# A graph network on one core: inverse counts in the near rows, folds in place of a reduce, and three and two near tiles by turns

## What is computed

```python
x_j = node_features[col]                                   # 100000 x 16
m = silu(einsum('ei,ej,ijh->eh', x_j, edge_attr_8, W_msg_tp) / sqrt(16 * 8))
agg = segment_sum(m @ W_msg_lin / sqrt(16), row, n_nodes)
```

```python
cnt = zeros((num_nodes, 8)).at[dst, edge_type].add(1.0)
norm = 1.0 / maximum(cnt[dst, edge_type], 1.0)             # one number for each edge
agg = segment_sum(msg * norm[:, None], dst, num_nodes)
```

## Time and profile before

| | |
|---|---|
| median of three runs | 4680.27 us |
| the profiled execution, whole | 4656.31 us |
| its span | 4654.4 us |
| TensorE busy, matmuls | 4430.5 us (95%) |
| VectorE busy | 4185.4 us (90%) |
| ScalarE busy | 3232.3 us (69%) |
| GpSimd busy | 3395.2 us (73%) |
| mean granted clock of TensorE | 0.981 of full |

### The profile page before, as it was taken

How to read it: one execution, slowest core, us unless ns; L and a number is a source line. 1 busy time by engine, 2 the same in 40 slices (tenths; PEclk the granted TensorE clock), 3 DMA queues, 4 the chain that set the end, 5 groups by cost and what they waited for, 6 DMA issues and landing times.

```text
span 4654.4 us, 106164 instructions
## 1 busy us (share of the span) xinstructions
PE 4430.5 (95%) x29576; PEld 3072.3 (66%) x29576; DVE 4185.4 (90%) x11965; ACT 3232.3 (69%) x5459; POOL 3395.2 (73%) x2615
## 2 busy tenths in 40 slices
PE   4999999999997999999988999999999999799998
PEld 3677777777774444444436777776777777566665
DVE  5999999999997999999987999997999999789887
ACT  4777777777774666666645777775777777577776
POOL 4888888888874888888845767665767676587886
PEclk8999999999997999999999999999999999899999
DMA  2111111111112222222212111111111111111111
GB/s 68 20 18 18 17 18 18 18 17 18 18 16 54 57 58 57 58 58 57 58 33 42 27 27 27 27 27 37 27 27 27 27 27 27 26 31 31 31 31 24
DMA packets 344557, 152.04 MB, mean 33 GB/s; under 512 B 268541, under 2 KB 329033, under 8 KB 344393
## 3 DMA queue, kind: packets, MB, share of 16 engines
q0 software_dynamic: 112000, 66.23, 10.5%
q1 hardware_dynamic: 232517, 85.33, 7.4%
HBM read 138.72 MB, written 9.77 MB: 32 GB/s over the span
## 4 chain that ended last, share of the span: by engine, by line
PE 79%; DVE 9%; issue 5%; DMA 3%; ACT 1%; POOL 1%; SPq 1%; DVEq 0%; POOLq 0%; ACTq 0%
PE acc L599 37%; PE rows_ps L756 15%; PE bank L692 13%; PE bank L772 4%; PE bank L764 2%; PE counts L606 2%; PE rows_ps L680 2%; DMA fields_all<-table_l,row_numbers 2%; DVE raw L1443 1%; PE counts L603 1%; PE eaT_ps L668 1%; POOL fields_all L583 1%; DVE stationary L1236 1%; DVE raw L1260 1%; DVE one_hot L1208 1%
## 5 line engine op out<-in xcount | busy, mean ns | idle before, releaser
L599 PE MATMUL acc<-one_hot,stationary 125*128 125x392 bf16 x12000 | 2343.7, 330 | 54.6 <-issue 28.3
L583 POOL DMA_INDIRECT gathered<-table_l,row_numbers x1200 | 1599.9, 1333 | 464.2 <-issue 356.0
L599 PEld LDWEIGHTS acc<-one_hot,stationary 125*128 125x128 bf16 x12000 | 1109.1, 99 | 755.3 <-issue 135.6
L867 ACT ACTIVATE distances<-count_hi,fields 125x392 bf16<-125x392 f16 (+1 forms) x2500 | 1222.5, 557 | 0.0
L1236 DVE TENSOR_TENSOR stationary<-mask,parts 125x1024 bf16<-125x1024 bf16 x1500 | 945.1, 684 | 0.2 <-ACT mask L852 0.2
L583 POOL DMA_INDIRECT fields_all<-table_l,row_numbers x600 | 765.9, 1277 | 237.8 <-issue 152.2
L852 ACT CAST mask<-is_lo 125x1024 bf16<-125x1024 f32 x500 | 521.7, 1043 | 460.1 <-issue 302.5
L1208 DVE TENSOR_SCALAR one_hot<-count_hi,fields 125x392 bf16<-125x392 f16 x2300 | 728.9, 342 | 13.5 <-issue 13.5
L692 PE MATMUL bank<-w,h1T 128*125 128x256 f32 x3200 | 717.2, 382 | 12.0 <-DVE product L1253 9.0
L583 POOL DMA_INDIRECT gathered<-table_l2a,row_numbers x400 | 511.4, 1279 | 288.3 <-DVE parts L1218 124.5
L756 PE MATMUL rows_ps<-node_parts,h1T 125*125 125x192 bf16 (+1 forms) x7200 | 679.4, 252 | 26.7 <-DVE node_parts L1287 19.5
(11 more groups left out here) (212 smaller groups left out, 4046.8 us busy)
## 6 DMA issues: line engine op xcount, KB each, us to landing
near_key<-near_keys_by_chunk SPq DMA_DIRECT2D x300, 122.1 KB
gathered<-table_l,row_numbers POOLq DMA_INDIRECT x1200
fields<-edge_fields SPq DMA_DIRECT2D x500, 31.2 KB
fields_all<-table_l,row_numbers POOLq DMA_INDIRECT x600
gathered<-table_l2a,row_numbers POOLq DMA_INDIRECT x400
gathered<-table_l2b,row_numbers POOLq DMA_INDIRECT x400
ea<-in_edge_attr SPq DMA_DIRECT2D x100, 62.5 KB
near_key<-near_keys_by_chunk SPq DMA_DIRECT2D x100, 61.0 KB
```

The costliest lines, as they stand in the source:

```text
L583: pool.indirect_dma_start(out=gathered[ph][:, s, t, :], in_=table[ph], out_offset=None, in_offset=bass.IndirectOffsetOnAxis(ap=row_numbers ...
L599: mm = pe.matmul(acc[:, :], stationary[:, s, k, t, :, :].rearrange("p a b -> p (a b)"), one_hot[:, s, t, :], start=first and t == 0 and k ...
L867: ins = act.activation(distances[:, i * n:(i + 1) * n], count_hi[:, 0:n], ACT.Abs, scale=-1.0, bias=fields[:, s, k, t:t + 1].bitcast(F32))
```

## The change

It does four things, three of them in l1.

1. `NEAR_OF` has two numbers a phase, by parity of the chunk: in l1 even chunks have 3 near tiles and odd ones 2; other phases keep 4 and 4. Everything that used the number takes the parity. The PSUM room of the near rows is three banks, and the turned products go to the bank of `eaT_ps`, which only l0 used. A chunk has 7 near keys in place of 6.
2. The near rows of l1 carry inverse counts in place of counts. The reciprocal is written into the node rows and copied to the table stage. In `near_finish` the inverse counts are copied out of PSUM (`near_inverse`), the four count operations are gone, and the near types are not made there in l1.
3. In the body of l1 the inverse counts of the near tiles are multiplied by `is_type` of all 8 tiles, and one reduce makes `edge_norm` of 8 tiles.
4. The reduce into `raw` becomes three adds that fold 8 into 4, 2 and 1, with other steps of VectorE between them; the typed step now comes ahead of raw.

```diff
-NEAR_OF = {"l0": 0, "l1": 2, "l2a": 4, "l2b": 4, "l3": 4}
+NEAR_OF = {"l0": (0, 0), "l1": (3, 2), "l2a": (4, 4), "l2b": (4, 4), "l3": (4, 4)}
...
-        rows_ps = ctx.enter_context(nc.psum_tensor("rows_ps", [128, 2, 512], F32))
+        rows_ps = ctx.enter_context(nc.psum_tensor("rows_ps", [128, 3, 512], F32))
+        turned_ps = eaT_ps[:].rearrange("p t e -> p (t e)").bitcast(F32)
...
-            "l1": ("is_lo", "raw", "typed", "hi", "weighed", "rest", "rows_read", "mid", "low"),
+            "l1": ("is_lo", "typed", "raw", "hi", "weighed", "rest", "rows_read", "mid", "low"),
...
-                    for t in range(far(ph)):
+                    for t in range(far(ph, s)):
...
-                    if ph != "l3" and follows(chunk, 3):
-                        near_rows(ph, chunk + 3)
+                    if ph != "l3" and follows(chunk, 3):
+                        near_rows(ph, chunk + 3, 1 - s)
...
-                if ph != "l3":
-                    near_types(ph, chunk)
+                if ph == "l2a" or ph == "l2b":
+                    near_types(ph, chunk, s)
...
-                    dve.tensor_tensor(near_is_type[:, 0:count], near_is_type[:, 0:count], rows[:, :, 0, F:ROW1],
-                                      ALU.mult).then_inc(near_counted, 1)
-                    factor = near_ea8[:, bass.ds(chunk, 1), :].rearrange("p c (t r) -> p (c t) r", t=count)
+                    dve.tensor_copy(near_inverse[:, s, 0:count], rows[:, :, 0, F:ROW1])
+                    factor = near_ea8[:, bass.ds(chunk, 1), :].rearrange("p c (t r) -> p (c t) r", t=NEAR1)[:, NEAR1 - count:]
...
-                if ph == "l1":
-                    dve.wait_ge(near_counted, 3 * chunk + 1)
-                    dve.tensor_reduce(near_count[:], near_is_type[:, 0:count], AX.X, ALU.add).then_inc(near_counted, 1)
-                    dve.wait_ge(near_counted, 3 * chunk + 2)
-                    dve.tensor_scalar(near_count[:], near_count[:], 1.0, None, ALU.max).then_inc(near_counted, 1)
-                    dve.wait_ge(near_counted, 3 * chunk + 3)
-                    dve.reciprocal(edge_norm[:, bass.ds(chunk * T + far("l1"), NEAR1)], near_count[:])
...
-            link(dve.tensor_copy(node_rows1[0:NP, :, F:ROW1], by_relation), "l1_rows_made")
             link(dve.tensor_reduce(stat[:], by_relation, AX.X, ALU.add))
             link(dve.tensor_scalar(cnt[:], cnt[:], 1.0, None, ALU.max))
-            dve.reciprocal(stage1[:, :, RELATIONS * F:], by_relation).then_inc(ev("inverse_counts"), 1)
+            link(dve.reciprocal(node_rows1[0:NP, :, F:ROW1], by_relation), "l1_rows_made")
+            dve.tensor_copy(stage1[:, :, RELATIONS * F:], node_rows1[0:NP, :, F:ROW1]).then_inc(ev("inverse_counts"), 1)
...
+                def fold(j):
+
+                    return dve.tensor_tensor(products[:, :, 0:j, :], products[:, :, 0:j, :], products[:, :, j:2 * j, :], ALU.add)
+
...
                 one_hots("l1", s, (0,))
-                dve.wait_ge(ev("l1_products"), chunk + 1)
-                st.mark(dve.tensor_reduce(raw[:, s, 0:far("l1")], product1[:, 0:far("l1")].rearrange("p t (j h) -> p t h j", h=F), AX.X, ALU.add))
+                dve.wait_ge(ev("l1_products"), 3 * chunk + 1)
+                fold(4).then_inc(ev("l1_products"), 1)
                 st.mark(matches(is_type[:], count_lo, s, TYPE, RELATIONS))
-                one_hots("l1", s, (1, 2))
+                dve.wait_ge(ev("l1_products"), 3 * chunk + 2)
+                fold(2).then_inc(ev("l1_products"), 1)
+                one_hots("l1", s, (1,))
+                dve.wait_ge(ev("l1_products"), 3 * chunk + 3)
+                st.mark(dve.tensor_tensor(raw[:, s, 0:n], products[:, :, 0, :], products[:, :, 1, :], ALU.add))
+                one_hots("l1", s, (2,))
                 dve.wait_ge(silu_ready, chunk + 1)
...
-                        st.mark(dve.tensor_tensor(is_type[:, 0:far("l1")], is_type[:, 0:far("l1")], gathered1[:, s, 0:far("l1"), RELATIONS * F:], ALU.mult))
+                        dve.tensor_tensor(is_type[:, n:T], is_type[:, n:T], near_inverse[:, s, 0:T - n], ALU.mult)
+                        st.mark(dve.tensor_tensor(is_type[:, 0:n], is_type[:, 0:n], gathered1[:, s, 0:n, RELATIONS * F:], ALU.mult))
...
-                        st.mark(dve.tensor_reduce(edge_norm[:, bass.ds(chunk * T, far("l1"))], is_type[:, 0:far("l1")], AX.X, ALU.add))
+                        st.mark(dve.tensor_reduce(edge_norm[:, bass.ds(chunk * T, T)], is_type[:], AX.X, ALU.add))
```

More of the change, by code:

```diff
@@ L276, in build, with far, keys_of @@
         near_done = sem("near_messages_ready")
-        near_counted = sem("near_counts_step")
-        def far(ph):
-            return T - NEAR_OF[ph]
+        def far(ph, s):
+            return T - NEAR_OF[ph][s]
         def chunks_before(ph):
             return CHUNKS * NEAR_PHASES.index(ph)
-        def keys_of(ph):
-            return slice(NEARS, KEYS) if ph == "l1" else slice(0, NEARS)
+        def keys_of(ph, s):
+            end = KEYS if ph == "l1" else NEARS
+            return slice(end - NEAR_OF[ph][s], end)
         distances_ready = sem("distances_ready")
@@ L759, in near_rows, with near_turn @@
                 mm.then_inc(near_gathered, 1)
-            def near_turn(ph, chunk):
+            def near_turn(ph, chunk, s):
                 pe.wait_ge(near_outers, chunks_before(ph) + chunk + 1)
-                for t in range(NEAR_OF[ph]):
-                    mm = pe.transpose(bank[TURNED_BANK][:, t * EP:(t + 1) * EP],
+                for t in range(NEAR_OF[ph][s]):
+                    mm = pe.transpose(turned_ps[:, t * EP:(t + 1) * EP],
                                       near_outer[:, t, :, :].rearrange("p r f -> p (r f)"), ident[0:EP, 0:EP])
@@ L1287, in split_nodes, with near_types @@
                 link(dve.tensor_tensor(part[2], left, part[1], ALU.subtract), event)
-            def near_types(ph, chunk):
-                n = NEAR_OF[ph]
-                number = (near_type1 if ph == "l1" else near_type)[:, bass.ds(chunk, 1), :].rearrange("p c j -> p (c j)")
+            def near_types(ph, chunk, s):
+                n = NEAR_OF[ph][s]
+                number = near_type[:, bass.ds(chunk, 1), :].rearrange("p c j -> p (c j)")
+                number = number[:, number.shape[1] - n:]
                 dve.tensor_tensor(near_is_type[:, 0:n], count_key[:, None, 0:LO].to_broadcast([EP, n, LO]),
@@ L1312, in fill @@
                         near_begin(ph, chunk + 1, pair + s, 1 - s, (g,))
-                count, before_this = NEAR_OF[ph], chunks_before(ph) + chunk
-                rows = near_rows_ps[ph]
+                count, before_this = NEAR_OF[ph][s], chunks_before(ph) + chunk
+                rows = near_rows_ps[ph][:, 0:count]
                 width = ROW1 if ph == "l1" else F
```

75 lines of the change are left out of this document (38 added, 37 removed).

## The result

| | before | after |
|---|---|---|
| median, 7 runs each | 4679.73 us (4674.23 to 4683.43) | 4696.11 us (4690.18 to 4698.23) |
| ratio | | 1.0034, 95% interval 1.0025 to 1.0044 |
| profiled execution, span | 4654.4 us | 4688.4 us |
| on another chip, ratio | | 1.0059, interval 1.0042 to 1.0076 |

The change makes the kernel slower, by 16 us in the first measurement and 26 us in the second (4644.89 to 4670.66). I forecast +28, 4708 us, with a range over the cases of 4686 to 4724; 4696.11 lies within it, but outside the forecast's own 4699 to 4718 and inside the 4684 to 4698 of rival (b).

A forecast was written before the change was run, and what follows sets the result against it. GpSimd's gathers paced l1 at 9.48 us a chunk, TensorE 9.17 and VectorE 9.13 close behind; TensorE would pace at 9.73. l1 +26, setup +1, head +1 made +28 on 4680.27: 4708 us, range 4686 to 4724.

The forecast's parts named there:

- rival (b): Timed runs' extra 24 us lie in gather-paced stretches, so the difference shrinks to +4 to +18 us, 4684 to 4698; 13%.
- TensorE's 9.17: TensorE's own issue time in an l1 chunk of 9.46 us, summed from instruction starts; GpSimd 9.48, VectorE 9.13.
- TensorE's third tile: In every second l1 chunk, near rows, turn and messages of one more tile cost TensorE 1.12 us, +0.56 a chunk.
- the start wait: TensorE's 0.29 us idle ahead of an l1 chunk's first tile closes, leaving its own 9.73 as the period.
- rival (c): Uneven l1 chunks make a new wait, TensorE keeping 0.1 to 0.2 us idle: +10 to +20 more, 4718 to 4728; 12%.
- 97 chunks x (9.73 - 9.46): l1's growth: the new TensorE-paced period less the old period, over 97 chunks, +26 us.
- Setup and head (+2): Work ahead of the phases, a seventh near key among it, +1 us, and the head of l1, +1 us.
- -0.48 - 0.7 - 0.13 + 0.12: VectorE's terms per l1 chunk: folds, count operations gone, near_types gone, small multiply of inverse counts added, in us.
- the line: VectorE's fp32 cost, 0.155 + 1.05 ns an element, giving the three adds replacing the raw reduce 0.52, 0.34, 0.25 us.
- a wait for the silu: VectorE in l1, with less work between raw and the activation's result, may wait 0.2 us for it.
- no limit either: VectorE's need per l1 chunk falls from 9.13 to about 8.3 us, so it doesn't pace.
- (a): Third tile nearly hidden, under 0.58 us: the l1 period falls towards 9.17, 28 us less, 4652; 6%.

The follow-up runs named there:

- wide counts on the kernel before: The kernel before, with l1's matmul into counts given 128 columns of weights in place of 8: ratio 0.9995 to before.
- three tiles throughout, wide counts: The changed kernel with three near tiles in every l1 chunk and 128 columns of weights for the counts matmul: 4560.95 us, ratio 0.9800 to before.
- the second pair: The kernel before and the changed kernel, both profiled and timed again without an edit: 4644.89 and 4670.66 us, ratio 1.0059.
- two-and-two kernel: The changed kernel with l1's near tiles back to two in every chunk, VectorE's share of the change (parts 2 to 4) kept: ratio 1.0039 to before.
- the changed kernel with wide counts: The changed kernel with l1's matmul into counts given 128 columns of weights in place of 8: ratios 0.9922 and 0.9917 to before.
- two and one tiles: The changed kernel with two and one near tiles by turns in l1, in place of three and two: ratio 1.0208 to before.

## Why the prediction was right, and where it was off

**What bounds the kernel.** Right. GpSimd paced (wide counts on the kernel before bring nothing), TensorE's 9.17 stood right behind (three and two tiles give 9.717), and with both relieved (three tiles throughout, wide counts) the period is 8.49, again TensorE's own sum. The wide counts on the kernel before leave TensorE a lower granted clock, 0.95 in the stretch, and still nothing changes.

**TensorE's third tile.** Right: 1.09 us measured for 1.12, period 9.717 for 9.73. That the start wait would close was right too; the slack of ScalarE's and VectorE's chain was enough, and rival (c), new waits from uneven chunks, didn't come.

**The sum.** +28 forecast; l1 in the profiles is +17.7 and +19.6, the whole timed +16.4 and +25.8. The step that was off is "97 chunks x (9.73 - 9.46)". Chunks 8 to 92 give 84 x 0.250 = +21.0. The last seven give -2.9: once no near rows are left to make, TensorE has less to do and the end runs at 8.18 and 6.89 us, where the gathers had held the old kernel at 9.91 and 9.28. The first eight give -0.2, with a first period of 9.81 for 11.61, since the first chunks have one gather less. I had multiplied one period by nearly all chunks, which is about 8 us too much. In the second pair the same three parts give +21.6, -3.5 and +0.4, and the head of l1 +1.1. Setup and head (+2) gave nothing that stands out: the end of l0 came 1.7 us earlier in the first pair and 2.6 later in the second. So the mechanism was right and this term was over-sized, and that the second measurement came within 2 us of +28 is in part luck: its profiles differ by 22.0.

**VectorE.** The direction was right, the size not. In the two-and-two kernel its need is 8.4 us, 0.7 below 9.13; my terms for that kernel (-0.48 - 0.7 - 0.13 + 0.12) give 1.2 less, 7.9. The folds cost what the line gave, 0.56, 0.35 and 0.24 us. Other operations grew that I had left alone: the near one-hots of 250 elements take 0.376 us in place of 0.288, twice a chunk, and the halving of 96 elements 0.404 in place of 0.276, together 0.30 us. What makes them longer stays open. In the changed kernel a wait for the silu appears as I wrote, but of 95.7 us ahead of L1219 in 90.5 chunks (74.0 by the view for the silu, 21.7 without a releaser), 1.06 each and not 0.2: ScalarE does the silu behind TensorE's turn, so a VectorE that is early waits longer there. It costs nothing. The word that it is "no limit either" left out what it does to others: I took 1.58 us as the price of a gather whatever VectorE does. Alone, the vector part makes the gathers 1.60 and the kernel 0.39% slower. In the changed kernel this is covered by TensorE.

**The rivals.** (a), the hidden tile, fell: 1.09 us a tile, far above the 0.58 where it would turn. (b), that timed gather-paced stretches are slower than in the profile of before, is open. For it: in the first measurement the kernel before timed 24 us above its profile, the changed one 6 us, and the measured +16 is inside its +4 to +18. The first profile of the changed kernel is one of these slow timings (4690.18 us); against its repeat l2a is 6.4 us longer, l2b 3.5 and l3 15.5, but l1, where TensorE paces, 0.2 shorter. Against it: in the second measurement the medians agree with the profiled executions within 4 us and the difference is 26 us. The profiled execution of before, 4656.31, lies outside its own timed runs (4674.23 to 4683.43) and among the medians of the same kernel on other chips (4644.89, 4649.76, 4656.68), so a difference between chips or conditions, which I had not listed, is as good an account of the 24 us. No timed run of before has stages, so where they lay can't be said.

**The chances.** They don't quite add up: the forecast and (c) are 0.81, and more than half of (b) would bring "slower" to 0.88 or more and not 0.85.

## What to carry to other kernels

Before relieving the engine that paces, add up the issue time of the next one from starts, not from its busy share: here 9.17 in 9.46 us left room for 0.3, and the edit put 0.56 on it. Look in that sum for a term that is dearer than its size (the matmul with 8 columns of weights made a tile 0.86 us long, with 128 columns it is 0.66), because taking it away, with three tiles in every chunk, opened 2% where the move of work alone lost 0.3 to 0.6%. An engine freed from the path still changes when its operations meet another's. Multiply a period by the chunks that run at it, and count the first and last ones apart.

## What the runs showed of the hardware that was not expected

- An indirect DMA on GpSimd takes 1.21 us or up to 1.74 by where it starts against VectorE's products of bf16 tiles: 69 of 69 within 0.1 us behind the start of the first took 1.73 to 1.74, 120 just ahead of it 1.21 to 1.22. What it takes longer falls with what is left of the product (1.50 at 0.2 to 0.3 us into it, 1.31 at 0.4 to 0.5). Beside a reduce of 1.43 us with one input 92 of 92 took 1.21 to 1.22.
- More work on VectorE, 0.96 us a chunk, made a phase paced by gathers 12.6 us shorter than without it.
- A matmul with 8 columns of weights amid ones with 128: 0.259 and 0.262 us to its neighbours, with 128 columns 0.166. The 8 columns began to load 0.002 us ahead of their matmul, the 128 columns 0.164.
- TensorE's granted clock in l1, beside its busy time in the 880 us: 0.95 with wide counts on the kernel before (742.6 us busy), 0.97 in the changed kernel with wide counts (802.0), 0.92 with two and one tiles (796.4), and 1.00 in the kernel before (862.4) and the changed one (880.0). In the first three, matmuls into acc start up to 0.327 us apart in place of 0.166, which is the lower of the clock's two levels, 1.2 and not 2.4 GHz.
